# First attention: the two kinds of score matmul alternate in two halves of the TensorE array, from terms loaded twice

## What is computed

```python
h = _layernorm(x, axis=-1) * (1 + ca) + sa          # b, 256, 128
q = h @ Wq.T + bq;  k = h @ Wk.T + bk;  v = h @ Wv.T + bv
q, k, v = heads of 8 channels each                  # b, 16, 256, 8
q = apply_rope(q) * scale;  k = apply_rope(k)
dots = jnp.einsum('bnih,bnjh->bnij', q, k)
dots = jnp.where(i[:, None] < i[None, :], -100000.0, dots)
attn = jax.nn.softmax(dots, axis=-1)
o = jnp.einsum('bnij,bnjh->bnih', attn, v)
x = x + ga * (o.transpose(0, 2, 1, 3).reshape(b, 256, 128) @ Wo.T + bo)
```

## Time and profile before

| What | Value |
|---|---|
| Median of the timed runs | 1368.03 us (1363.39 to 1371.96) |
| The profiled execution | 1355.89 us, span 1354.0 us |
| Mean granted TensorE clock in it | 0.882 of full |
| TensorE matmul / weight load busy | 82% / 48% |
| VectorE / ScalarE / GpSimd busy | 60% / 36% / 22% |

### The profile page before, as it was taken

One profiled execution on the slowest core, in us unless ns is written; L12 is line 12 of the kernel. 1 busy time (PEld: TensorE's weight loads), 2 busy tenths in 40 slices (PEclk: granted clock), 3 DMA queues, 4 the chain that ended last, 5 costly groups with the idle time before them and its releaser, 6 DMA issues. The chain is left out here.

```text
span 1354.0 us, 25150 instructions
## 1 busy us (share of the span) xinstructions
PE 1105.7 (82%) x9345; PEld 654.5 (48%) x9345; DVE 815.0 (60%) x1910; ACT 483.5 (36%) x839; POOL 298.3 (22%) x283
## 2 busy tenths in 40 slices
PE   3699999999999599999999996588888889845140
PEld 2235454544444244444444442376777667744130
DVE  4456666646552466566666653488888888646322
ACT  0024444424445133323323321455555564411020
POOL 4132323213210000000000002342332321015536
PEclk9969999959999699999999998589999999855575
DMA  4534242422420622321332230323223322040233
GB/s 128 143 97 96 51 95 49 94 48 49 96 51 3 230 80 94 104 90 63 124 96 95 62 126 0 111 80 97 78 68 96 96 65 81 1 125 26 71 105 85
DMA packets 83989, 113.38 MB, mean 84 GB/s; under 512 B 9658, under 2 KB 53616, under 8 KB 81664
## 3 DMA queue, kind: packets, MB, share of 16 engines
q1 hardware_dynamic: 81840, 108.65, 28.5%
q0 software_dynamic: 2048, 3.37, 0.9%
HBM read 80.18 MB, written 32.65 MB: 83 GB/s over the span
## 5 line engine op out<-in xcount | busy, mean ns | idle before, releaser
L672 DVE TENSOR_REDUCE a_nmax<-ps 128x2 f32<-128x512 f32 (+1 forms) x192 | 132.4, 691 | 127.7 <-PE ps L513 88.2
L437 ACT ACTIVATE a_pr<-ps 128x512 f32<-128x512 f32 x192 | 114.2, 597 | 173.9 <-PE ps L488 124.9
L861 ACT ACTIVATE e_sg<-ps 128x512 f32<-128x512 f32 x136 | 81.2, 597 | 244.6 <-PE ps L886 231.5
L1050 DVE TENSOR_TENSOR e_up<-e_sg,ps 128x512 f32<-128x512 f32 x128 | 88.0, 687 | 106.9 <-PE ps L893 100.9
L886 PE MATMUL ps<-e_hT,e_wg 128*128 128x512 f32 x272 | 140.8, 600 | 0.8 <-DVE e_wT L1037 0.8
L902 PE MATMUL ps<-e_hm,e_wd 128*128 128x512 f32 x272 | 139.2, 594 | 1.4 <-DVE e_hm L1053 0.7
L472 PE MATMUL ps<-a_mask,identb 128*128 128x256 bf16 (+1 forms) x384 | 129.1, 336 | 13.5 <-DMA a_ks<-a_terms_d 9.4
L893 PE MATMUL ps<-e_hT,e_wu 128*128 128x512 f32 x272 | 139.8, 596 | 0.0
L1053 DVE TENSOR_TENSOR e_hm<-e_up,e_wb 128x512 f32<-128x512 f32 x128 | 88.5, 692 | 5.6
L902 PEld LDWEIGHTS ps<-e_hm,e_wd 128*128 128x128 f32 x272 | 51.5, 190 | 67.3 <-issue 63.5
L893 PEld LDWEIGHTS ps<-e_hT,e_wu 128*128 128x128 f32 x272 | 52.1, 191 | 65.6 <-issue 59.8
(11 more groups left out here) (266 smaller groups left out, 2031.6 us busy)
## 6 DMA issues: line engine op xcount, KB each, us to landing
e_wb<-e_wT_d SPq DMA_DIRECT2D x128, 256.0 KB, 3.3
a_gw<-a_gd_d SPq DMA_DIRECT2D x16, 1024.0 KB, 5.0
a_gd_d<-a_gc SPq DMA_DIRECT2D x64, 132.0 KB, 2.3
a_terms_d<-a_parts SPq DMA_DIRECT2D x32, 192.0 KB, 2.1
a_qs<-a_terms_d SPq DMA_DIRECT2D x16, 384.0 KB, 5.0
a_ks<-a_terms_d SPq DMA_DIRECT2D x16, 384.0 KB, 6.0
a_terms_d<-a_parts SPq DMA_DIRECT2D x32, 128.0 KB, 2.1
a_terms_d<-a_parts SPq DMA_DIRECT2D x32, 64.0 KB, 1.8
```

Source lines behind the costliest of these rows:

```text
L437: nc.scalar.activation(dst, src, ACT.Exp).then_inc(exp_done, 1)
L672: nc.vector.tensor_reduce(dst, src, AX_X, ALU.max, negate=True).then_inc(m_read, 1)
L861: nc.scalar.activation(sg[:, par], ps[:, 2 + par], ACT.Silu).then_inc(silu_done, 1)
L1050: nc.vector.tensor_tensor(up[:, par], sg[:, par], ps[:, 4 + par], ALU.mult).then_inc(up_done, 1)
```

## The change

`a0_qs` and `a0_ks` grow to 64 + 48 rows. The 48 rows of terms are loaded twice, to partition 64 (`M_ROW`) and to partition 0, so `spread` now counts four loads per batch. C scores read rows 0 to 50, M scores read rows 64 to 111 and name the array position (64, 0). The lists of C and M steps become one list of pairs: `scores(g, n, stage, gm)` first opens both banks with their mask matmuls (with the waits of both), then alternates C and M matmuls head by head. The pairs stand where the C steps stood, or near it; `turn_normal` moves ahead of the pair of C(2, 0), and `turn_max` directly behind `project(1)`.

```diff
@@ buffers
-                         "ks": nb("a0_ks", [A0_ROWS, 3, H, L], BF16)}
+                         "ks": nb("a0_ks", [M_ROW + HD * len(A0_TERMS), 3, H, L], BF16)}
-        qs = sb("qs", [TOP + 3, 3, H, L], BF16)
+        qs = sb("qs", [M_ROW + ROWS, 3, H, L], BF16)
-        STORE, SPREAD = 16 * len(RUNS), 16 * 2
+        STORE, SPREAD = 16 * len(RUNS), 16 * 4
@@ spread_parts
                     sp.wait_ge(done, b.x * STORE + STORE)
-                    sp.dma_start(dst[0:ROWS, b.k % 3].rearrange("p h n -> p (h n)"),
-                                 terms_d[side].rearrange("t (d h) n -> (t d) (h n)", h=H)).then_inc(spread, 16)
+                    for row in (M_ROW, 0):
+                        sp.dma_start(dst[row:row + ROWS, b.k % 3].rearrange("p h n -> p (h n)"),
+                                     terms_d[side].rearrange("t (d h) n -> (t d) (h n)", h=H)).then_inc(spread, 16)
@@ the score steps of TensorE
+            def score_m(g, n, a, b):
+                p, bank = b.k % 3, ps[:, (3 * g + n) % 2]
+                h = HG * ((2 * n if n < 2 else 0) + a) + g
+                out = bank.rearrange("p (a n) -> p a n", a=count_of(n))[:, a]
+                mm = nc.tensor.matmul(out, qs[M_ROW:M_ROW + ROWS, p, h, P:L] if n < 2 else qs[M_ROW:M_ROW + ROWS, p, h, 0:P],
+                                      ks[M_ROW:M_ROW + ROWS, p, h, :] if n < 2 else ks[M_ROW:M_ROW + ROWS, p, h, 0:P],
+                                      start=False, stop=(a == count_of(n) - 1), skip_group_check=True,
+                                      tile_position=(M_ROW, 0))
+                if a == count_of(n) - 1:
                     mm.then_inc(m_full, 1)
...
+            def scores(g, n, stage, gm):
+                ahead = {"M": 1, "N": 2}[stage]
+                def step(b):
+                    m = b + ahead
+                    has_c, has_m = 0 <= b.k < B, 0 <= m.k < B
+                    if has_c:
+                        open_c(g, n)(b)
+                    if has_m:
+                        open_m(gm, n)(m)
+                    for a in range(count_of(n)):
+                        if has_c:
+                            score_c(g, n, a, b)
+                        if has_m:
+                            score_m(gm, n, a, m)
                 return step
@@ the list of TensorE, the middle of it
-                     ("C", outputs(0)), ("D", turn_outputs(1)), ("A", project(0)), ("C", scores_c(2, 0)),
-                     ("D", turn_normal), ("N", scores_m(0, 0)), ("A", project(1)), ("C", scores_c(2, 1)),
-                     ("M", turn_max), ("N", scores_m(0, 1)), ("C", scores_c(2, 2)), ("N", scores_m(0, 2)),
+                     ("C", outputs(0)), ("D", turn_outputs(1)), ("A", project(0)), ("D", turn_normal),
+                     ("B", scores(2, 0, "N", 0)), ("A", project(1)), ("M", turn_max),
+                     ("B", scores(2, 1, "N", 0)), ("B", scores(2, 2, "N", 0)),
```

More of the change, by code:

```diff
@@ L41 @@
 A0_ROWS = HD * len(A0_TERMS) + 3
+M_ROW = 64
 X_PARTS = [(0, 2), (2, 5), (5, B)]
@@ L351, in body @@
                 for stage, step in order:
+                    if stage == "B":
+                        step(b)
+                        continue
                     c = b + ahead[stage]
@@ L472, in causal, with open_c @@
                 nc.tensor.matmul(out, identb[:], mask[:, form, 0:n], start=True, stop=False, skip_group_check=True)
-            def scores_c(g, n):
+            def open_c(g, n):
                 def step(b):
-                    p = b.k % 3
                     if g == 0 and n == 0:
@@ L482, in step, with open_m @@
                     if n < 2:
[L484 to L489, removed]
-                    else:
[L491 to L497, removed]
+                        causal(bank.rearrange("p (j n) -> p j n", j=2)[:, :, 0:P], 1, 2)
+                    else:
+                        causal(bank.rearrange("p (j n) -> p j n", j=HJ), 1, HJ)
                 return step
-            def scores_m(g, n):
+            def open_m(g, n):
                 def step(b):
-                    p = b.k % 3
                     if g == 0 and n == 0:
@@ L522, in step, with count_of, score_c @@
-                    mm.then_inc(m_full, 1)
+                        causal(bank.rearrange("p (j n) -> p j n", j=2)[:, :, P:L], 0, 2)
+                    else:
+                        causal(bank.rearrange("p (j n) -> p j n", j=HJ), 0, HJ)
+                return step
+            def count_of(n):
+                return 2 if n < 2 else HJ
+            def score_c(g, n, a, b):
+                p, bank = b.k % 3, ps[:, 2 + (3 * g + n) % 2]
+                h = HG * ((2 * n if n < 2 else 0) + a) + g
+                out = bank.rearrange("p (a n) -> p a n", a=count_of(n))[:, a]
+                mm = nc.tensor.matmul(out, ks[0:TOP + 3, p, h, 0:P] if n < 2 else ks[0:TOP + 3, p, h, P:L],
+                                      qs[0:TOP + 3, p, h, :] if n < 2 else qs[0:TOP + 3, p, h, P:L],
+                                      start=False, stop=(a == count_of(n) - 1), skip_group_check=True)
+                if a == count_of(n) - 1:
+                    mm.then_inc(c_full, 1)
@@ new lines, in score_m @@
+            def score_m(g, n, a, b):
+                p, bank = b.k % 3, ps[:, (3 * g + n) % 2]
+                h = HG * ((2 * n if n < 2 else 0) + a) + g
+                out = bank.rearrange("p (a n) -> p a n", a=count_of(n))[:, a]
+                mm = nc.tensor.matmul(out, qs[M_ROW:M_ROW + ROWS, p, h, P:L] if n < 2 else qs[M_ROW:M_ROW + ROWS, p, h, 0:P],
+                                      ks[M_ROW:M_ROW + ROWS, p, h, :] if n < 2 else ks[M_ROW:M_ROW + ROWS, p, h, 0:P],
+                                      start=False, stop=(a == count_of(n) - 1), skip_group_check=True,
+                                      tile_position=(M_ROW, 0))
+                if a == count_of(n) - 1:
+                    mm.then_inc(m_full, 1)
@@ L604, in turn_back @@
                 mm.then_inc(d_full, 1)
[L606 to L609, removed]
-                     ("C", outputs(0)), ("D", turn_outputs(1)), ("A", project(0)), ("C", scores_c(2, 0)),
-                     ("D", turn_normal), ("N", scores_m(0, 0)), ("A", project(1)), ("C", scores_c(2, 1)),
-                     ("M", turn_max), ("N", scores_m(0, 1)), ("C", scores_c(2, 2)), ("N", scores_m(0, 2)),
-                     ("C", outputs(1)), ("D", project_out), ("C", scores_c(3, 0)), ("N", scores_m(1, 0)),
-                     ("C", scores_c(3, 1)), ("N", scores_m(1, 1)), ("D", turn_back), ("C", scores_c(3, 2)),
-                     ("N", scores_m(1, 2)), ("C", outputs(2))])
+            run(pe, [("B", scores(0, 0, "M", 2)), ("B", scores(0, 1, "M", 2)), ("B", scores(0, 2, "M", 2)),
+                     ("D", outputs(3)), ("S", project(2)),
+                     ("B", scores(1, 0, "M", 3)), ("D", turn_outputs(0)), ("B", scores(1, 1, "M", 3)),
+                     ("A", turn_tokens), ("B", scores(1, 2, "M", 3)),
+                     ("C", outputs(0)), ("D", turn_outputs(1)), ("A", project(0)), ("D", turn_normal),
+                     ("B", scores(2, 0, "N", 0)), ("A", project(1)), ("M", turn_max),
+                     ("B", scores(2, 1, "N", 0)), ("B", scores(2, 2, "N", 0)),
+                     ("C", outputs(1)), ("D", project_out),
+                     ("B", scores(3, 0, "N", 1)), ("B", scores(3, 1, "N", 1)), ("D", turn_back),
+                     ("B", scores(3, 2, "N", 1)), ("C", outputs(2))])
         @block.vector
```

## The result

The changed kernel took 1433.39 us (median of 4 runs, 1432.49 to 1434.79); the kernel before, in the same turn on the same chip, took 1369.99 (4 runs, 1363.39 to 1373.55). The ratio is 1.0469, with a 95% interval of 1.0426 to 1.0513: slower by nearly 5%, 63 us. The forecast was 1406, its range 1349 to 1450. The span of the profiled execution is 1430.8 us, 76.8 above that of before; this is more than 63 because the profiled execution of before was a quick one.

What follows compares the result with a forecast made beforehand. PE sets the pace, with the loop through the terms' reload under 1 us behind and binding after the change. Loop +18.5, clock +17.7, filling +7, end −5, total +38: 1394 profiled, 1406 as median; range 1349 to 1450.

Steps and rivals of the forecast that it cites:

- The second loop: Split on POOL, terms to DRAM and back, M scores, next split: 22.46 us per batch, under 1 us of slack.
- Work on PE: PE's work per batch in the first attention falls by 5.0 us, to 16.9; a pair takes 0.63 us.
- that rival: Row strips of C and M scores don't overlap: each pair costs 0.21 us more, 1416 us; chance 0.09.
- The turn of the maxima: On PE, now directly behind the projection, it waits 1.14 us for DVE's second rotation, where 0.54 were left before.
- The spread: Four copies of 384 KB per batch instead of two, awaited by the first M step: landing 3.0 us later.
- if each takes its turn: Bound for the landing of the terms: copies one after another, 2.3 us apart, so two more add 4.6 us.
- The rival of two halves side by side: Copies into both partition halves load together, landing 0.3 us later: 1349 us as a median; chance 0.16.
- The rest of the loop: From the first M step to the end of the next split: 10.6 us, against 11.13 before.
- The clock: PE's idle before the first M step lowers its clock: 3 long dips, 9 short, of 12 batches; net +17.7 us.
- The fill: Filling the pipeline: the first batches wait for the later-landing terms with nothing to hide it, +7 us.
- The end: The last two batches of the stage need no load of terms and gain on PE: −5 us.
- "low clock" rival: PE's clock stays low in most batches, 9 long dips and 3 short: +45 in place of 17.7, 1433 us; chance 0.15.

Runs made afterwards that it cites:

- experiments of 1 and 3: Kernel before plus unread copies into rows 64 to 111: ratio 1.0616; changed kernel with upper copies issued first, first M step waiting for these alone: ratio 1.0022.
- experiment 4: Changed kernel with upper copies first and awaited alone, plus turn of the maxima one pair later: 1332.91 us; that later turn alone on the changed kernel: 1411.2 us.
- experiments of 1: Kernel before with two extra, unread copies on the awaited count: into rows 64 to 111, 1455.39 us; into a spare buffer in rows 0 to 47, 1466.9 us.
- experiment 6: Changed kernel with twenty filler mask matmuls before the load wait: 1420.68 us; eight fillers, with upper copies awaited alone and the maxima turn later: 1319.68 us.
- second kernel of experiment 2: Changed kernel keeping pairs and new order, but both scores read rows 0 to 50 from one load: 1374.81 us, ratio 1.0091.
- experiment 2: Here its first kernel: changed kernel loading the upper half in the first three batches only, later M scores reading old terms: 1364.44 us, ratio 1.0021.

## Why the prediction was right, and what was off

**The bound and the direction: right.** The second loop, with under 1 us of slack, was the one that counted. PE idle before the first M mask, released by ks, came in every batch, 6.35 us in the batch shown. The experiments of 1 and 3 show the cause from both sides: the extra copies alone, with the old PE code, bring the loss (+6.2%), and the same copies off the wait take it away (+0.2%).

**Work on PE: right.** A pair takes 0.65 us (0.63 forecast), so the strips overlap and that rival falls. In the batches at full clock of experiment 4 PE is busy 16.8 us (16.9 forecast). The turn of the maxima waits 0.97 us (1.14 forecast). The wait of a pair for DVE is 0.7 us once a batch (1 forecast).

**The spread: the term that was mis-sized.** I took +3.0 us; it was 14.9 − 10.37 = +4.5. That is the bound "if each takes its turn" (4.6), which I had from the landings of the two copies. I leaned instead on the rate of the first microsecond in the earlier trace rows and took off "a little overlap" on top. The rival of two halves side by side, with its +0.3, falls with the experiments of 1: the other half wins about 1 us of more than 4. The rule of the Trainium skill in "SBUF — State Buffer", section "Door 1: The DMA port swizzle", says which ports each half reaches. That copies of one queue would use both sets at once was my inference, not the rule, and the runs speak against it; whether the 1 us comes from the ports is not shown.

**The rest of the loop: right.** 10.6 us, confirmed at full clock by 25.44 (experiment 6: 10.4 + 4.5 + 10.6 = 25.5) and by 20.43 (experiment 4, against 20.3).

**The clock: right in kind, wrong in form.** I dealt out 3 long dips and 9 short ones. Instead every batch has one, of some 10 to 12 us at half clock (my estimate from 0.79 to 0.82 over 27 to 30 us), and pays on average 28.45 − 25.5 = 3.0 us. Over thirteen periods that is 38 us. The kernel before paid 308.10 − 13 x 22.46 = 16 over the same thirteen, so the net is +22, against +17.7 forecast. That the sizes are near each other is partly luck, since the dips behind them are of another kind. One reading was wrong as well: the clock slice that I took for one "after 377 us" is the fourteenth, which begins at 440 us, near the end of the stage. A second short dip did come in the stage, at about 400 us (mean clock 0.95 from 377.46 to 444), so the count held, but not by that slice.

**The fill: right** (+8.2 against +7). **The end: wrong in sign.** I gave −5 for "the last two batches need no spread". One was counted too many: the last split still has to land, and PE stands 6.84 us for it at 471.04. The end cost +3.0.

On the profiled executions the sum is: loop 13 x (25.5 − 22.46) = 39.5, clock 22, fill 8, end 3, and 4 outside the stage, together 76.8. The forecast was 38. Of the 39 missing, 21 are the loop (the mis-sized spread, over thirteen periods and not twelve), 8 the end, 4 to 5 the clock, 1 the fill, 4 outside. As medians 27 of them are seen, because I placed the kernel after 12 us above its profiled execution, as before was; it lies at it. So 12 us of the error in the steps are hidden in the medians by luck. The "low clock" rival gave 1433, the measured time, but not by its steps: it kept the +3.0.

**Open.** What fixes the length of a dip. The runs show that less idle in PE before and behind the load goes with a higher clock, and filler in a gap of 2 us with a full one, in the same loop; they don't show how large a gap is free. Small gaps alone don't settle it: in the second kernel of experiment 2 PE stood at most 1.2 us for the load from 200 to 360 us, and two of its seven batches from 203 to 364 us still had a mean clock of 0.75. Why filler did not keep the clock in the changed kernel, where the gap is three times as long, is not known; PE still waited up to 2.8 us behind it. No run issues the copies from a second queue, so what is said of the halves holds for one queue.

## What to carry to other kernels

A saving on the engine that looks full is worth no more than the slack of the loop behind it. Work out that loop from one batch's timeline first, and if the change puts more copies on the awaited transfer, price them one after the other. When a transfer must grow, let the first consumer wait only for its own copies: here that alone was worth 62 us of the profiled span with all the traffic left in. Idle time on TensorE cost twice here, once as such and once in the clock behind it, and a small wait near it weighed more than its own length.

## What the runs showed of the hardware that was not expected

Four copies of 384 KB, two into each half of the partitions, issued by one queue, had landed 14.6 us after the split; all four into the same half 15.6 us; two copies 10.4. Moving a wait of half a microsecond changed the time by 30 us and the mean clock from 160 to 340 us from 0.86 to 0.97. And a kernel with less work on PE (experiment 2, 0.86 from 160 to 340 us) had a lower clock there than the kernel before with more work (0.92 in the same stretch), so that two microseconds of waiting per batch and one microsecond of a shorter loop cancelled.
